# Layer norm of six batches moved from ScalarE to GpSimd, and thirteen more matrix products whose results nobody reads

## The reference

```python
x = L0_attn_x                                     # (8, 512, 128)
x = _layernorm(x + _L0_attn_ref(x, ...))          # gated attention; only 32 chosen tokens differ from a common row
x = _layernorm(x + _L0_ffn_ref(x, ...))           # the part below

# _L0_ffn_ref
x = x + _mla(_rmsnorm(x, g1), Wq, Wdkv, Wuk, Wuv, Wo)   # causal attention, 16 heads of 8
x = x + _moe(_rmsnorm(x, g2), gate_w, w1, w2)           # 8 experts of 256, the best 2 of each token
```

## Time and profile before

| | before |
|---|---|
| time, median of three executions | 659.99 us |
| lowest and highest | 656.0 and 661.51 us |
| the profiled execution: time | 654.62 us |
| the profiled execution: span of the trace | 652.7 us |
| its mean granted TensorE clock | 0.971 |
| PE, DVE, ACT, POOL busy | 95%, 79%, 63%, 38% |

### The profile page before, as it was taken

How to read it: one execution, slowest core, us unless ns; L and a number is a source line. 1 busy time by engine, 2 the same in 40 slices (tenths; PEclk the granted TensorE clock), 3 DMA queues, 4 the chain that set the end, 5 groups by cost and what they waited for, 6 DMA issues and landing times. The chain is left out here.

```text
span 652.7 us, 14245 instructions
## 1 busy us (share of the span) xinstructions
PE 623.0 (95%) x4928; PEld 410.5 (63%) x4928; DVE 515.9 (79%) x1903; ACT 409.4 (63%) x747; POOL 250.2 (38%) x317
## 2 busy tenths in 40 slices
PE   8999898998899999999999999999999999999996
PEld 4576544464466666666666666766666666666885
DVE  3756889757688899878888789888978888873666
ACT  3663467375667576857586668675867566755443
POOL 8130423122323365335334533353334333543442
PEclk9999989589799999999999999999999999999998
DMA  8700000000000000000000000000000000000000
GB/s 308 222 15 22 1 4 2 3 2 3 2 2 3 3 3 2 19 2 4 2 19 2 2 4 12 9 2 3 19 3 2 3 18 3 2 3 18 1 17 16
DMA packets 15191, 12.67 MB, mean 19 GB/s; under 512 B 6729, under 2 KB 13330, under 8 KB 14866
## 3 DMA queue, kind: packets, MB, share of 16 engines
q1 hardware_dynamic: 14370, 11.78, 5.8%
q10 hardware_dynamic: 752, 0.01, 0.1%
HBM read 9.16 MB, written 2.10 MB: 17 GB/s over the span
## 5 line engine op out<-in xcount | busy, mean ns | idle before, releaser
L1234 ACT ACTIVATE prob<-psW 128x1024 f32<-128x1024 f32 (+1 forms) x192 | 183.1, 954 | 105.9 <-PE psW L1100 105.3
L1326 DVE CUSTOM_DVE_ANT_0 psS<-psS,maskb 128x128 f32<-128x128 f32 (+1 forms) x498 | 232.1, 518 | 20.2 <-PE psS L1082 17.6
L911 POOL TENSOR_SCALAR_AFFINE_SELECT prob<-prob 128x512 f32<-128x512 f32 x128 | 80.4, 638 | 220.2 <-ACT prob L1234 220.2
L1058 PE MATMUL turn<-wexp,late 128*128 128x128 f32 x1016 | 126.5, 278 | 0.4 <-DVE late L1390 0.4
L1058 PEld LDWEIGHTS turn<-wexp,late 128*128 128x128 f32 x1016 | 118.9, 192 | 5.6 <-issue 3.6
L1196 ACT ACTIVATE late<-turn 128x512 f32<-128x512 f32 x128 | 76.3, 597 | 62.9 <-PE turn L1050 53.4
L1082 PE MATMUL psS<-kT,qT 24*128 24x256 f32 (+1 forms) x498 | 108.2, 414 | 6.2 <-DVE top L1326 5.7
L1390 DVE SCALAR_TENSOR_TENSOR late<-late,turn 128x512 f32<-128x512 f32 x128 | 87.3, 683 | 33.4 <-ACT late L1196 32.6
L1100 PE MATMUL psW<-qT,kT 26*128 26x256 f32 (+2 forms) x512 | 94.7, 407 | 6.7 <-ACT prob L1234 6.5
L922 POOL TENSOR_TENSOR late<-late 128x512 f32<-128x512 f32 x62 | 79.8, 1287 | 53.8 <-DVE late L1419 46.9
L1112 PE MATMUL psV<-prob,va 128*32 128x512 f32 (+3 forms) x1024 | 92.0, 455 | 0.3 <-POOL prob L911 0.3
(11 more groups left out here) (273 smaller groups left out, 854.1 us busy)
## 6 DMA issues: line engine op xcount, KB each, us to landing
qT<-shiftT SPq DMA_DIRECT2D x256, 2.0 KB
prob<-in_xT SPq DMA_DIRECT2D x4, 512.0 KB, 6.3
X<-in_x SPq DMA_DIRECT2D x1, 2048.0 KB, 15.8
out<-late SPq DMA_DIRECT2D x8, 256.0 KB, 2.4
prob<-in_wqkvT SPq DMA_DIRECT2D x1, 1024.0 KB
late<-in_w SPq DMA_DIRECT2D x1, 1024.0 KB, 10.5
prob<-in_wqkvT SPq DMA_DIRECT2D x2, 256.0 KB, 3.5
late<-in_woutT SPq DMA_DIRECT2D x1, 512.0 KB
```

The costliest lines, as they stand in the source:

```text
L911: pool.affine_select(out=blk, in_=blk, compare_op=ALU.is_ge, fill=0.0, base=0, pattern=[[0, 4], [1, P]], channel_multiplier=-1).then_inc(s ...
L1058: last = mm(into[:, D * c:D * c + D], hid[:, n % 2, k, P * c:P * c + P], wexp2[:, n, k, :], start=(k == 0), stop=(k == 1))
L1234: A(into, src, ACT.Exp).then_inc(s["exp_ready"], 1)
L1326: last = V.tensor_tensor_reduce(at, at, maskb[:, T - P * (c + 1):T], 1.0, BIG, ALU.add, ALU.max, top[:, u % 2, c, 2 * p + j:2 * p + j + 1])
```

## The change

In the list `order`, "normalize" of batches 2 to 7 keeps its place, but POOL does it instead of ACT, in two instructions over all 512 tokens: `X * rs1`, and after a wait on its own semaphore `X + off1`. Batches 0 and 1 stay on ACT. `UNREAD_AT` gets thirteen more places (78 instead of 65): 2.6, 3.3, 3.6, 4.6, 5.1 and 22.6, 23.1, 24.2, 24.3, 25.2, 25.3, 25.9, 26.02.

```diff
@@ UNREAD_AT @@
-    7.02, 9.02, 9.02, 11.94, 12.02, 13.02, 14.02, 15.02, 15.02, 16.02, 18.02, 19.02, 22.02, 23.52, 24.94, 25.02,
+    22.02, 22.6, 23.1, 23.52, 24.2, 24.3, 24.94, 25.02, 25.2, 25.3, 25.9, 26.02, 27.02, 28.02, 31.02, 31.52, 31.52,
@@ block.gpsimd @@
+                elif what == "normalize" and b >= 2:
+                    pool.wait_ge(s["off1_ready"], b + 1)
+                    xb = X[:, C * b:C * b + C, :]
+                    own(pool.tensor_tensor(xb, xb, rs1[:, b % 4, 0, :].unsqueeze(2).broadcast_to([P, C, D]), ALU.mult))
+                    pool.tensor_tensor(xb, xb, off1[:, b % 4, :].unsqueeze(2).broadcast_to([P, C, D]),
+                                       ALU.add).then_inc(s["x_ready"], 1)
@@ block.scalar @@
-                if what == "normalize":
+                if what == "normalize" and b < 2:
                     act.wait_ge(s["off1_ready"], b + 1)
```

## The result

| | before | after |
|---|---|---|
| time, median of 17 executions each | 659.99 us | 662.51 us |
| lowest and highest | 656.0 and 664.44 us | 659.34 and 667.51 us |
| the profiled execution: time, span | 654.62, 652.7 us | 662.51, 660.5 us |
| its mean granted clock | 0.971 | 0.964 |

The ratio of the times is 1.0049, with a 95% interval of 1.003 to 1.0068: the change makes the kernel 0.5% slower. I had forecast 656.0 us. The sign was wrong, and the time lies 0.5 us above the range. Here and in the experiments the intervals leave out six slow executions, one of the kernel before at 919.27 us, one of pool_5to7 at 1013.09 us and four that lie over 1.5% above the fastest of their kernel, while the medians hold all and the columns on half clock leave out the first two alone.

What follows compares the result with a forecast made beforehand. It took PE, nearly gapless, as the bound, with DVE nearly full ahead of two half-clock stretches. Terms: -2.0 (ACT) + 0 (POOL) + 1.0 (products) - 3.0 (clock) = -4.0, from 659.99 to 656.0 us; range 649 to 662.

Steps and rivals of the forecast that it cites:

- The POOL step: On POOL the pair costs 2.1 us, at most 2.5; batch 2's third mask has 0.7 us slack: cost 0.
- the term for the meeting with VectorE: POOL's pair sharing SBUF interfaces with VectorE: cost on DVE's side taken as 0, at most 0.3 us.
- The second half-clock stretch: 161.3 to 171.6 us, behind batch 4: half clock more likely gone than not, gaining 3.0 us.
- ACT, batch 4: PE's weight step at 160.29 us could start earlier, but scores need DVE's maxima: gain 0.7 us, at most 2.1.
- ACT, batch 2: At 101.27 us, DVE's one gap behind it is the gain: 0.4 us.
- Batches 5 to 7: PE's gaps of 0.37 and 0.74 us behind batches 5 and 7 go: gain 0.9 us, at most 1.1.
- The unread products: Thirteen more on PE at 0.22 us each: cost 1.0 us, between 0 (hidden behind DVE) and 2.9.
- First stretch: 113.5 to 134.0 us: half clock more likely to stay; its going would gain 5.0 us at most.
- The profile against the median: Median 5.4 us above the profiled execution; more half clock in timed executions would explain it, but no row showed it.
- the slower one: At slots 5.7 to 7.5 the pair takes 3.1 us, a mask is late, the clock falls: 665.6 us, chance 0.13.
- the likeliest case: Half clock at 161.3 to 171.6 us goes, that at 113.5 to 134.0 stays: 656.0 us, chance 0.38.

Runs made afterwards that it cites:

- pool_5to7: The kernel before with "normalize" of batches 5 to 7 alone moved to POOL, no products added: 663.71 us, ratio 1.0062.
- after_shifted: The changed kernel with the POOL pairs of batches 4 to 7 placed behind the nearest "shift": 653.07 us, ratio 0.9919.
- both_mended: The kernel before with batches 2 to 7 on POOL, 4 to 7 behind "shift", and thirteen products, four moved behind the score step: 654.17 us.
- act_later_apart: The kernel before with ACT's "normalize" of batches 2 to 7 1.5 slots later, and thirteen products, four moved behind the score step: 655.93 us.
- after_again: The changed kernel timed once more, unaltered: 663.18 us, ratio 1.0062.
- after_apart: The changed kernel with four products moved from between weight and score step to behind the score step: 665.27 us, ratio 1.0111.
- pool_after_shift: The kernel before with "normalize" of batches 2 to 7 on POOL, 4 to 7 behind the nearest "shift", no products added: 653.45 us.
- act_later: The kernel before with ACT's "normalize" of batches 2 to 7 1.5 slots later in its queue: 654.43 us, ratio 0.9907.
- pool_only: The kernel before with "normalize" of batches 2 to 7 moved to POOL, no products added: 657.19 us, ratio 0.998.
- pool_2to4: The kernel before with "normalize" of batches 2 to 4 alone moved to POOL, no products added: 654.29 us, ratio 0.9909.
- products_only: The kernel before with the thirteen unread products added and nothing else: 659.97 us, ratio 1.0012.
- products_apart: The kernel before with the thirteen unread products, four of them moved to just behind the score step: 660.32 us, ratio 1.0004.

## Why the prediction was wrong, step by step

- **The POOL step failed.** The price of the pair was right: 1.04 and 1.04 us, with 1.42 for the first at batch 6 alone, and no "value" step waited for a mask at slot 7. The mask ran at 109.75 and the values at 110.96:

```profile
107.64 1.04 POOL L879 TENSOR_TENSOR X<-X,rs 128x512 f32<-128x512 f32 x1
108.76 1.04 POOL L880 TENSOR_TENSOR X<-X,off 128x512 f32<-128x512 f32 x1
109.75 0.64 POOL L918 TENSOR_SCALAR_AFFINE_SELECT prob<-prob 128x512 f32<-128x512 f32 x1
...
110.96 0.86 PE L1119 MATMUL psV<-prob,va 128*32 128x256 f32 x16
```

  What failed is the term for the meeting with VectorE, "I take 0, at most 0.3 us". I looked at DVE's bulk, L1326, and not at which DVE instruction has two SBUF inputs beside the pair. It is short (0.19 us), stands once in six slots, and the scores hang on it. I read the contention as a dearer instruction, when it is a wait for the other's end. The earlier trace rows would have shown it: L922 begins 0.02 us behind DVE's 0.68 us and takes 0.54 us more than its 1.27. Turned around, a 0.19 us instruction behind a 1.04 us one would take about 1 us. The term was 9.4 us of the median, not 0: after against after_shifted is 3.7 us at equal clock, and 20 us of half clock besides, some 6 us by the slope.
- **The second half-clock stretch** was worth what I said, and more: with both parts and "shift" free, the kernels gain 4.0 to 4.3 us between slots 24 and 34 (after_shifted -4.04, both_mended -4.34, act_later_apart -4.34); I had 0.7 + 3.0 for batch 4 and the clock, less a part of the products' 1.0. In these three profiles no half clock stands from 140 to 190. With the pair beside "shift" (after, after_again, after_apart) it fell at 166 to 169, 3 of 3. So the step failed only through the one above. With the relief at batch 4 or the products alone it fell too, between 162 and 169, in all six: in these profiles both parts were needed. That is one profile a kernel, and the mean half clock hardly bears it out: with the relief alone it is 36.8 us (pool_after_shift) and 35.6 (act_later), with the products as well 35.5 and 34.7. That the products hold the clock up where the relief is there is thus not shown.
- **ACT, batch 4**: 0.7 us forecast, at most 2.1; slots 24 to 26 gave 3.1 in each kernel without the products (pool_only, act_later, pool_after_shift, pool_2to4). But of this 1.9 to 4.2 us go back in the next two slots, where the scores wait for DVE, as I had argued, only later. In pool_only:

```profile
163.18 1.42 PE L1088 MATMUL psS<-kT,qT 24*128 24x256 f32 x4 [1.41 <-DVE top L1332]
```

  No PE wait for ACT stands at slot 26 of after, as forecast.
- **ACT, batch 2**: from slot 4 to 8 after gains 0.07 and products_only loses 0.33, which makes 0.4, as forecast. **Batches 5 to 7**: 0.9 forecast; from slot 34 to 102 after_shifted gains 0.24. PE's gap closes, and opens again a few slots on.
- **The unread products**: +1.0 forecast, 0 to 2.9. At equal clock products_only measures +3.9, above my upper bound. Outside they cost the 0.2 us each that I had; the four between a weight and a score product cost 0.5 to 0.6 more each in the kernel before and between slots 22 and 26 of after, which the working had no term for. On the kernel before this is repaid by 11 us less half clock.
- **First stretch**: I expected it to stay at 113.5 to 134. It came in two pieces, 118 to 126 and 131 to 136, and varies from profile to profile (3.4 us of half clock in act_later_apart, 23.9 in products_apart). A reading of one profile can't carry a term of 5 us here. The stretch at half clock that ends the span of before was 3.3 us long, not 2; PE has no work in it.
- **The profile against the median**: "that the timed executions hold more half clock than the profiled one" was right: 48.1 against 37.9 us, which is 3.1 of the 5.4 us.
- **The rivals**: the slower one, at 665.6 us, had the right engine and the right pair of instructions, but the wrong victim: a mask, which had slack, and not the maxima, which have none. Its 665.6 us is 3.1 us too much. With "shift" free the change comes out faster, as the likeliest case had it, but not by its terms: after_shifted gains 0.2 us on before at equal clock, where ACT and the products were to give 1.0, and some 5.8 by half clock, where the second stretch was to give 3.0.

## What to carry to other kernels

When work moves to GpSimd, list the VectorE instructions that will run beside it and read SBUF, the short ones too, and ask what hangs on each; count nearly the whole rest of the instruction that began first as the wait (1.04 us for 0.19; for L922 0.54 of a rest of 0.66). If one of them feeds the critical engine, place the moved work right behind it with a wait on its semaphore: that was worth 9.4 us of 662.5 here. And before moving work off a queue that blocks a critical step, try it later in the same queue: act_later did about as well (654.43 us) by two changed lines.

## What the hardware showed that I had not expected

- A 128x16 VectorE instruction of 0.19 us takes 1.04 us beside a GpSimd instruction, and so does one with a single tensor as input, up to 0.77 instead of 0.18. GpSimd's masks hold it up as well as its additions.
- Two products that share the array, one behind the other in the queue, lose their overlap by a full-height product of 0.2 us between them: 0.5 to 0.6 us more there, though not always in the whole time.
- One short wait on PE (1.2 us, at 260.04) is followed by a fall of the clock at 261.6. All five kernels with the pair of batch 6 beside "shift" fell between 261.0 and 265.7, and none of the other nine did between 190 and 300. The mean half clock of a kernel went from 28.9 us (after_shifted) to 59.4 (after_apart), which is 9 us by the slope of 0.30: more than any single term of the sum.
